# Two-layer graph network on one core: the last tile of each round of 64 is gathered row by row by the sync engine

## The reference, cut to what matters

```python
h = jnp.maximum(_layernorm(x, axis=-1), 0.0)
W_rel = jnp.einsum('rb,bio->rio', w_comp, weight)      # 64 relations, 16 bases
h_all = jnp.einsum('ni,rio->nro', h, W_rel)
msg = h_all[src, etypes] * norm
agg = jax.ops.segment_sum(msg, dst, num_segments=N)
out = x + relu(agg + h_bias + h @ loop_weight)
```

## Time and profile before

| | |
|---|---|
| median of 3 runs | 975.67 us |
| profiled execution | 974.94 us, span 973.4 us |
| TensorE busy (matmuls) | 787.6 us, 81% |
| VectorE busy | 710.2 us, 73% |
| ScalarE busy | 355.6 us, 37% |
| GpSimd busy | 487.2 us, 50% |
| L662 on GpSimd, 391 gathers | 370.3 us busy |
| L1275 on TensorE | 303.1 us busy |
| L975 and L972 on VectorE | 279.7 and 148.4 us busy |

### The profile page before, as it was taken

One profiled execution on the slowest core, in us unless ns is written; L12 is line 12 of the kernel. 1 busy time (PEld: TensorE's weight loads), 2 busy tenths in 40 slices (PEclk: granted clock), 3 DMA queues, 4 the chain that ended last, 5 costly groups with the idle time before them and its releaser, 6 DMA issues.

```text
span 973.4 us, 27338 instructions
## 1 busy us (share of the span) xinstructions
PE 787.6 (81%) x5974; PEld 584.6 (60%) x5975; DVE 710.2 (73%) x2380; ACT 355.6 (37%) x705; POOL 487.2 (50%) x609
## 2 busy tenths in 40 slices
PE   6577667667879999997189889898888888887877
PEld 4254333334549999996067667666666666655545
DVE  7999999997635645346077677776778877887885
ACT  1424668998740000013054444433433332222100
POOL 2145433420018300101577777777777777777772
PEclk9699999998659999998589999999999999999999
DMA  4024456994320000114932121211212222221213
GB/s 124 24 81 104 124 145 152 161 167 115 95 68 2 1 1 2 34 55 116 324 85 54 51 54 52 53 52 52 54 51 54 52 54 51 53 53 52 53 52 88
DMA packets 64856, 73.33 MB, mean 75 GB/s; under 512 B 12805, under 2 KB 53180, under 8 KB 64670
## 3 DMA queue, kind: packets, MB, share of 16 engines
q1 hardware_dynamic: 48366, 37.31, 15.5%
q0 software_dynamic: 16432, 35.29, 14.4%
HBM read 43.85 MB, written 8.22 MB: 53 GB/s over the span
## 4 chain that ended last, share of the span: by engine, by line
PE 33%; DVE 25%; issue 15%; DVEq 10%; POOL 8%; DMA 5%; ACT 2%; SPq 1%; POOLq 0%; ACTq 0%
PE ps L1198 15%; PE ps L1275 9%; POOL CT L662 8%; DVE ohbuf L829 6%; DVE CT L972 5%; PE ps L1106 4%; DMA CT<-h_dram,src_col 4%; DVE CT L975 3%; DVEq L975 3%; DVE u L829 3%; DVEq L128 3%; PE ps L1254 2%; DVEq L972 2%; DVE ohbuf L824 1%; ACT stage L1355 1%
## 5 line engine op out<-in xcount | busy, mean ns | idle before, releaser
L662 POOL DMA_INDIRECT CT<-h_dram,src_col x391 | 370.3, 947 | 125.1 <-issue 102.5
L1275 PE MATMUL ps<-CT 128*128 128x256 f32 x1180 | 303.1, 405 | 64.4 <-DVE CT L972 31.3
L1275 PEld LDWEIGHTS ps<-CT 128*128 128x128 f32 x1180 | 202.8, 191 | 158.9 <-issue 142.2
L975 DVE SCALAR_TENSOR_TENSOR CT<-ps,dlP,CT 128x256 f32<-128x256 f32 x580 | 279.7, 482 | 4.3
L972 DVE COPY CT<-CT 128x128 f32 x590 | 148.4, 252 | 124.5 <-PE ps L1275 57.9
L1417 ACT COPY CT<-ps 128x256 f32<-128x256 f32 x200 | 77.6, 388 | 306.3 <-PE ps L1275 302.6
L1106 PE MATMUL ps<-ohbuf 128*128 128x400 bf16 x395 | 104.8, 374 | 37.4 <-DVE ohbuf L829 14.8
L1198 PE MATMUL ps<-u,CT 128*128 128x192 bf16 x1250 | 105.0, 246 | 1.7 <-DVEq L937 0.9
L1355 ACT CAST stage<-ps 128x800 bf16<-128x800 f32 x100 | 82.3, 823 | 63.5 <-PE ps L1106 62.5
L1198 PEld LDWEIGHTS ps<-u,CT 128*128 128x128 bf16 x1250 | 103.0, 98 | 2.9 <-DVEq L901 1.3
L1254 PE MATMUL ps<-CT 128*128 x800 | 95.8, 277 | 6.8 <-ACT CT L1417 4.6
(11 more groups left out here) (184 smaller groups left out, 647.6 us busy)
## 6 DMA issues: line engine op xcount, KB each, us to landing
CT<-stage SPq DMA_DIRECT2D x200, 100.0 KB, 3.5
u<-types_dram POOLq DMA_DIRECT2D x49, 128.0 KB, 3.5
CT<-h_dram,src_col POOLq DMA_INDIRECT x391, 2.5
coef_dram<-coef_out POOLq DMA_DIRECT2D x49, 64.0 KB, 4.0
CT<-coef_dram SPq DMA_DIRECT2D x1, 3048.0 KB, 12.0
out<-CT SPq DMA_DIRECT2D x4, 256.0 KB
ohbuf<-x SPq DMA_DIRECT2D x3, 320.0 KB, 3.8
x_dram<-ohbuf SPq DMA_DIRECT2D x3, 320.0 KB, 2.4
```

Of the source, the lines that this page charges most:

```text
L662: pool.indirect_dma_start(out=gring[:, (j + 1) % GRING, :], out_offset=None, in_=h2_dram, in_offset=bass.IndirectOffsetOnAxis(ap=src_col[: ...
L975: dve.scalar_tensor_tensor(kpair[:, u, :, :], nodes.unsqueeze(1).broadcast_to([P, BASES, WIN]), dl, coef_flat[:, ds(tiles * -BASES + NT * ...
L1275: pe.matmul(ps[:, ds(summed.place(counts[u][0], RING), 1), 0:WIN * BASES], gpair[:, u, :], kpair[:, u, :, :].rearrange("p b d -> p (b d)") ...
```

## The change

SP gathers the last tile of each round of 64 (gathers 63, 127, ... 383), row by row: 128 DMAs of one row each, from h2_dram at a row number held in a register, into partition e of the ring's place 0. GpSimd leaves these six gathers out. The row numbers (six times 128 of src) are loaded into src_row once, between the first layer's x loads and its x2 stores. In the stage SP loads eight numbers at a time into registers. Rows are spread over the round: none for tiles 0 to 3, then some two behind each announced tile, up to tile 62; after that SP waits for all 128 and announces the tile. From the second round on, SP waits after announcing tile 4 until VectorE has used the tile of 64 gathers before in place 0. The first round stands in straight code ahead of the aligned loop.

```diff
@@ sync
+            sp.wait_ge(rel_tables, 1)
+            for k in range(ROUNDS):
+                tile = NT - (k + 1) * GRING
+                sp.dma_start(src_row[:, k * P:(k + 1) * P], src[tile * P:(tile + 1) * P].unsqueeze(0)).then_inc(rows_in, 16)
...
-            sp.addr_align(BLOCK, offset=0, max_nops=0)
-            with sp.Fori(0, NT // GRING) as k:
-                for i in range(GRING):
+            sp.wait_ge(rows_in, 16 * (ROUNDS + 1))
...
+            def rows_after(i):
+                return max(i - ROWS_FROM + 1, 0) * P // (GRING - 1 - ROWS_FROM)
+            def gather_rows(k, lo, hi):
+                for e in range(lo, hi):
+                    if e % ROW_REGS == 0:
+                        first = k * P + e
+                        rows_of[:] = [sp.alloc_register(f"row{next(numbers)}") for _ in range(ROW_REGS)]
+                        sp.load(rows_of, src_row[0:1, slice(first, first + ROW_REGS) if isinstance(first, int) else ds(first, ROW_REGS)])
+                    row = sp.snap(rows_of[e % ROW_REGS], donate=True, min_val=0, max_val=N - 1)
+                    sp.dma_start(gring[e:e + 1, 0, :], h2_dram[ds(row, 1), :]).then_inc(row_in[e % ROW_SEMS], 16)
+            def round_of_tiles(k):
+                for i in range(GRING - 1):
                     sp.wait_ge(g_in[i], (k + 1) * 16)
                     sp.sem_inc(gathered, 1)
+                    if i == ROWS_FROM and not (isinstance(k, int) and k == 0):
+                        sp.load(freed_at, tab_tile[0:1, ds(k * -GRING + NT, 1)])
+                        sp.wait_ge(pair_in, sp.snap(freed_at, min_val=1, max_val=2 * S))
+                    gather_rows(k, rows_after(i - 1), rows_after(i))
+                for i in range(ROW_SEMS):
+                    sp.wait_ge(row_in[i], (k + 1) * (16 * P // ROW_SEMS))
+                sp.sem_inc(gathered, 1)
+            round_of_tiles(0)
+            sp.addr_align(BLOCK, offset=0, max_nops=0)
+            with sp.Fori(1, ROUNDS) as k:
+                round_of_tiles(k)
@@ gpsimd
-            for j in range(GRING):
+            for j in range(GRING - 1):
                 gather(j)
...
                 for j in range(first, last + 1):
-                    gather(j)
+                    if j % GRING != GRING - 1:
+                        gather(j)
```

More of the change, by code:

```diff
@@ L91 @@
 GSTEP = 4
+ROUNDS = NT // GRING
+ROW_SEMS, ROW_REGS = 4, 8
+ROWS_FROM = 4
 BATCH = 5
@@ L344, in build @@
         begun = carve_stage(TURNS + 1)
+        src_row = stage_f[0:1, 2 * BATCH * HID:2 * BATCH * HID + ROUNDS * P].bitcast(I32)
         v_tmp = stage[:, :, :].rearrange("p r n -> p (r n)")[:, 0:4 * BATCH * HID].bitcast(F32)
@@ L421, in build @@
         h2_copied = sem("h2_copied")
-        g_in = [sem(f"g_in{i}") for i in range(GRING)]
+        g_in = [sem(f"g_in{i}") for i in range(GRING - 1)]
+        row_in = [sem(f"row_in{i}") for i in range(ROW_SEMS)]
         gathered = sem("gathered")
@@ L528, in _ @@
             sp.dma_start(x2[:], x2_dram.rearrange("(g p) f -> p g f", p=P)).then_inc(x2_in, 16)
-            sp.addr_align(BLOCK, offset=0, max_nops=0)
-            with sp.Fori(0, NT // GRING) as k:
-                for i in range(GRING):
+            sp.wait_ge(rows_in, 16 * (ROUNDS + 1))
+            numbers = itertools.count()
+            freed_at = sp.alloc_register("freed_at")
+            def rows_after(i):
+                return max(i - ROWS_FROM + 1, 0) * P // (GRING - 1 - ROWS_FROM)
+            rows_of = []
+            def gather_rows(k, lo, hi):
[8 more added lines that the diff above has]
+                for i in range(GRING - 1):
                     sp.wait_ge(g_in[i], (k + 1) * 16)
                     sp.sem_inc(gathered, 1)
+                    if i == ROWS_FROM and not (isinstance(k, int) and k == 0):
[9 more added lines that the diff above has]
+                round_of_tiles(k)
             for i in range(NT % GRING):
```

## The result

The changed kernel takes 1017.4 us (median of 4 runs, 1016.27 to 1019.0) against 976.08 before (four runs; the three named above gave 975.67): ratio 1.0431, 95% interval 1.0416 to 1.0445. The profiled execution took 1016.27 us, its span is 1014.4, which is 41.0 more than before.

A forecast was written before the change was run, and what follows sets the result against it. VectorE and TensorE were taken to bound the last stage, not GpSimd. SP's 73.6 us rounds outlast VectorE's rounds 3 to 5, adding 34 us to the profiled 974.94: 1009 us, range 981 to 1085.

The forecast's parts named there:

- GpSimd's six gathers: Last stage: leaving them out takes 7.5 us off GpSimd, which has 3.6 us to spare at the end; worth 0.
- The count of tiles from two lines' counts: Last stage: pairs (L972) minus window copies (L1417) gives tiles used; VectorE is 27 to 49 tiles behind GpSimd.
- three views that named GpSimd and its gathers: Chain of waits, GpSimd's unbroken line and the wait table; rival that GpSimd is the bound: 967.4 us, chance 0.06.
- The loads of row numbers: Six one-row DMAs on SP after the first x loads, 1.8 us, hidden before SP's next DMA.
- the earlier start: Round 0 before the aligned loop: VectorE starts up to 5 us earlier, but TensorE's first pair comes at 493.5; worth 0.
- The wait that decides: SP waits after tile 4 until VectorE begins the round, then has one VectorE round for everything; 34 us lost.
- The round's sum: SP's round: rows 58.9, loads 7.2, announcements 4.1, landing 2.4, last tile's pair 1.0; at least 73.6 us.
- the way back: End of SP's round: VectorE still has the last tile's own pair before SP is released again, 1.0 us.
- A register load with its arithmetic: SP's loads of eight row numbers, 16 per round: 0.45 us each with arithmetic and gaps, 7.2 us a round.
- a variant of a rival: Loop grown to some 490 instructions: a 5.3 us jump in each of three tight rounds, 16 us more, 1025; no separate chance.
- By round: SP's 73.6 us against VectorE's 71, 61.8 and 53.7 in rounds 3, 4 and 5; rounds 1 and 2 hidden.
- One row at a time: Rival: SP's rows share one path and each must land, 2.4 us, before the next; about 2400 us, chance 0.02.

The follow-up runs named there:

- the first run: Kernel before, with GpSimd leaving out the last gather of each round of 64 and SP announcing that tile without a wait: 975.74 us, ratio 0.9999.
- the two runs that take either half away: Changed kernel without row DMAs, their loads and the wait for them: 975.76 us; changed kernel with rows to a spare buffer, no wait for VectorE: 975.87 us.

## Why the prediction was right

Forecast 1009 us, range 981 to 1085; measured 1017.4.

- GpSimd's six gathers worth 0: right, by the first run alone. The count of tiles from two lines' counts decided against three views that named GpSimd and its gathers.
- The loads of row numbers and the earlier start worth 0: the loads are hidden; VectorE's round 2 ended 1.4 us sooner than before, about as much as runs differ, so the start is left at nothing shown.
- The wait that decides: right. It shows in the two runs that take either half away. What the prediction did not see is that SP, once late, meets the wait all but over: in rounds 4 and 5 SP stood in it for 0.13 us, and the round was SP's own sum.
- The round's sum, 73.6 predicted, 75 to 77 measured, was mis-sized in four terms that partly cancel, and that it came so close is in part luck: the loads took 5.9 us more, the way back 2.9 more, the rows some 3.8 less and the landing 1.4 less. (A slip besides: 59 announcements of 0.067 are 4.0 us and not 4.1.) A register load with its arithmetic: 0.45 predicted from ScalarE's load of four numbers, 0.687 + 0.051 and two gaps of 0.04 = 0.82 measured; 16 of them 13.1 us instead of 7.2. A row: 0.46 predicted; from the first row DMA of round 5 to the last are 994.5 - 923.4 = 71.1 us, less 15 loads (12.3) and 57 announcements (4.0) 54.8, over 127 steps 0.43. Of that 0.238 is the DMA, which a register address did not make dearer than L447's 0.25. The landing: 2.4 predicted, but about 1.0 from the end of SP's last issue (994.5 + 0.24) to the announcement at 995.8. The way back until SP is released: 1.0 predicted, for the last tile's own pair, 3.9 measured, 2.5 of it the branch. I had the branch as a variant of a rival, at 5.3.
- By round: 2.6, 11.8 and 19.9 us predicted, 6.3, 15.3 and 21.4 measured. 3.7, 3.5 and 1.5 us more in the three rounds, less the 1.4 us by which they begin sooner, is most of the 8 us between forecast and result.
- One row at a time: not seen. Rows were issued 0.43 us apart, and the last had landed about 1.0 us after its issue, so more than one was under way at a time. Whether all of them ran on one DMA engine, as the prediction took from the Trainium skill ("DMA: Bandwidth & Descriptors", section "Why a DMA increments its semaphore by 16 and not by 1"), no run here shows.
- The Trainium skill's rule that spreading DMAs over the engines may help where an engine is full of DMA slices ("Perfetto Trace Analysis", section "DMA Optimizations") has a condition, that descriptor generation is the bottleneck. GpSimd's row looked full, and the run with six gathers left out shows that the condition did not hold.

## What to carry to other kernels

An engine without a gap is not yet the bound: count what it has produced against what its consumer has used, and where the stock never runs out, cutting its work is worth nothing. Work placed behind a wait has only the time from that wait's end to its own deadline, so compare its sum with the shortest stretch between two releases and not with the mean. Losses of that kind bend: free up to the shortest stretch, then a full price in each stretch that is passed.

## What the runs showed that was not expected

- A register load on SP takes longer with more numbers: 0.43 us for one number (L567), 0.69 for 8 and 1.14 for 16 (medians). I had taken 0.31 from ScalarE's load of four.
- SP's way back through a loop of some 490 instructions took 2.5 to 3.0 us from the branch to the first instruction. It took 3.0 to 3.3 in the run with 96 rows, whose loop has 384 instructions, and 0.3 in the run with one register load, whose loop has 338. Why is not shown.
- In round 5 of the changed kernel the granted clock fell to a mean of 0.77 between its levels of 1.2 and 2.4 GHz while TensorE waited 21.7 us for VectorE's pairs. SP's own sum accounts for the round, so it cost nothing that shows.
